# Gated delta rule: triangular blocks inverted by substitution on 16 rows instead of 32, without the trip through DRAM

## The chip, the cores and the metric

The kernel is one program on one core of one Trainium2 chip. It runs on TensorE (PE), VectorE (DVE), ScalarE (ACT), GpSimd (POOL) and SyncE (SP), which here only issues DMAs. The metric is the device time of one execution in microseconds, smaller is better; it is given as the median of several runs of the same kernel.

## The reference, cut to what matters

The reference is a chain of eight layers on an input of 1024 tokens by 256 features. The third, a gated delta rule with 6 heads (key width 32, value width 64), is the only one that the change touches. Per head it is

```
def _step(S, xs):
    qt, kt, vt, gt, bt = xs
    S = S * jnp.exp(gt)[..., None, None]
    pred = jnp.einsum('bhk,bhkv->bhv', kt, S)
    delta = (vt - pred) * bt[..., None]
    S = S + jnp.einsum('bhk,bhv->bhkv', kt, delta)
    return (S, jnp.einsum('bhk,bhkv->bhv', qt, S))
```

followed by a normalization, a gate and an output projection. The order is token by token. The kernel computes it in chunks of 128 tokens: 8 chunks a head, 48 in all. Within a chunk the tokens' corrections depend on each other through a strictly lower triangular 128x128 matrix A, and what is needed is the inverse T = (I - A)^-1 (A with its sign) of each of the 48. Then W = T times the scaled keys, and a scan over the 8 chunks carries the state.

## The kernel before, in words

`build` calls the layers one after the other, and each ends in a barrier of all engines. Inside a layer each `nc.Block` holds one instruction list per engine, and a block ends in a barrier too. Engines wait for each other by semaphores; all orders are written out by hand.

`gated_delta` has these blocks in order: projections and convolution (L1119); norms and decay factors (L1235); the block that makes A and the score matrices (L1347), where DVE subtracts and masks, ACT takes exponents and DVE multiplies with the products in PSUM (psum), two heads a step, while POOL scales keys, queries and values; the **inversion block** (L1461); the scan (L1597); the output norm (L1677); and `project_out`. EA holds the 48 matrices A, transposed, with keys on the partitions.

The inversion goes from small diagonal blocks to large ones.

*Substitution.* The 128 rows fall into four diagonal blocks of 32 (`group(q)`), so there are 192 blocks of 32x32. `load_a_blocks` (SP) writes the diagonal blocks to a DRAM scratch and reads them back so that each partition holds one whole block: 128 partitions for the first four heads (group 0), 64 for the last two (group 1). `substitute` then goes through the rows: step i multiplies column i of A with row i of T so far (an outer product, L1063) and adds it to the rows below (L1067), 31 steps of two instructions with waits between. DVE does group 0 while POOL does group 1. A copy transposes each block (L1070), and `store_t_blocks` and seven more DMAs take T and its transpose through DRAM to where TensorE wants them: TT (transposed inverse) and T64.

*Merges.* Two inverted neighbours T1, T2 with the block A21 between them give the lower left block T2 A21 T1. `x32` computes X = A21 T1 for the pairs of 32-row blocks, ACT copies X to SBUF, `y32` multiplies by T2, DVE copies into TT and T64; `x64` and `y64` do the same for the pair of 64-row blocks. All go in three batches b of 16 chunks, in the order x32(b), x64(b-1), y32(b), y64(b-1), W(b-2). A small matmul works on the tile of the 128x128 array that its operands' partitions name: rows by those of its inputs, columns by those of its output. float32 matmuls show as two records each in the trace.

*W.* `w_features(b)` (L1491) computes for each head and half four matmuls of 128 rows into 32 columns, so one column tile at a time; ACT copies the result with a minus sign (`keep_w`, nWT), and TensorE waits for every second copy.

The scan block (L1597) starts with SP loading `own_block`; DVE waits for it before its first copy of U (L1650).

## Time and profile before

| | |
|---|---|
| median of three runs | 1583.32 us (1582.37 to 1586.07) |
| the profiled execution | 1582.23 us |
| its span, first to last instruction | 1580.5 us |
| busy in the span: PE, DVE, ACT, POOL | 1351.1, 937.7, 670.4, 255.8 us |
| mean granted TensorE clock | 0.894 of full speed |
| the inversion block | 477.9 to 577.0 us of the span |

The profiled execution is 1.7 us longer than its span, and the median lies 1.1 us above the profiled execution. PE stands for matmuls and PEld for its weight loads. Busy shares are means over layers with different limits; what counts for one block is which engine or transfer ends last in it. A granted clock of 1.0 is 2.4 GHz, 0.5 is 1.2 GHz.

### The profile page before, as it was taken

To read this page: it belongs to the slowest core of one execution; us is meant where nothing else is said; L and a number is where in the kernel's file an instruction comes from. 1 tells how busy PE (TensorE), PEld (TensorE's weight loads), DVE (VectorE), ACT (ScalarE), POOL (GpSimd) and SP (SyncE) were. 2 spreads that over 40 slices of the span, in tenths; PEclk is the share of its full clock that TensorE was granted. 3 is DMA by queue.
4 is the path that set the end of the run, shared out by engine and by line. 5 is a ranking of instruction groups with operands and counts; after the bars stand their busy time and mean duration, and the time that the engine had idled before them with its cause. 6 is when DMAs were issued, how large, how long until landed. Compare 5 with 4: busy or idle time off the path is not lost. (4 is left out here: it accounts for less than half of the span.)

```text
span 1580.5 us, 31133 instructions
## 1 busy us (share of the span) xinstructions
PE 1351.1 (85%) x12875; PEld 756.3 (48%) x12883; DVE 937.7 (59%) x2142; ACT 670.4 (42%) x948; POOL 255.8 (16%) x340
## 2 busy tenths in 40 slices
PE   7999993987380696698999998999689999998999
PEld 3355542463250675456355545435335555555436
DVE  3899958644689125573899955442345555534331
ACT  4577773634331121463577773210334444442110
POOL 4300000000126202003300000120234343210110
PEclk9899996998555588799999998999869999998999
DMA  3122102000310400001222103000300000000000
GB/s 91 28 42 38 27 15 98 0 12 0 100 17 23 77 5 0 14 1 30 50 42 35 30 4 95 0 1 9 60 8 14 17 12 17 7 3 1 0 0 27
DMA packets 51807, 41.64 MB, mean 26 GB/s; under 512 B 26497, under 2 KB 41970, under 8 KB 51666
## 3 DMA queue, kind: packets, MB, share of 16 engines
q1 hardware_dynamic: 51666, 39.65, 11.6%
q8 instruction: 102, 1.67, 0.4%
q14 instruction: 39, 0.32, 0.1%
HBM read 20.33 MB, written 3.43 MB: 15 GB/s over the span
## 5 line engine op out<-in xcount | busy, mean ns | idle before, releaser
L560 DVE TENSOR_REDUCE row_max_pieces<-psum 128x1 f32<-128x512 f32 (+3 forms) x672 | 406.7, 647 | 121.2 <-PE psum L455 119.0
L657 ACT ACTIVATE probs<-psum 128x1024 f32<-128x1024 f32 (+7 forms) x384 | 343.5, 899 | 220.2 <-PE psum L455 220.1
L509 PE MATMUL psum<-probs,v_ones 128*32 128x256 f32 (+1 forms) x2688 | 238.7, 376 | 6.4 <-POOL probs L444 4.1
L455 PE MATMUL psum<-q_all,k_head 97*32 97x512 f32 (+3 forms) x1536 | 192.4, 492 | 3.5 <-issue 3.5
L455 PE MATMUL psum<-k_stack,q_stack 96*32 96x512 bf16 x2048 | 163.1, 388 | 4.7 <-DVE row_max_pieces L560 2.3
L455 PE MATMUL psum<-q_stack,k_stack 97*32 97x512 bf16 x2048 | 160.1, 384 | 0.0
L509 PEld LDWEIGHTS psum<-probs,v_ones 128*32 128x32 f32 x2688 | 88.2, 109 | 81.7 <-POOL probs L444 21.1
L455 PE MATMUL psum<-k_head_bf,q_all_bf 80*32 80x512 bf16 (+3 forms) x768 | 96.1, 346 | 4.8 <-POOL q_all_bf L2281 3.4
L455 PEld LDWEIGHTS psum<-q_all,k_head 97*32 97x32 f32 x1536 | 78.8, 110 | 34.4 <-issue 8.5
L455 PEld LDWEIGHTS psum<-k_stack,q_stack 96*32 96x32 bf16 x2048 | 57.4, 97 | 73.4 <-DVE row_max_pieces L560 20.5
L455 PEld LDWEIGHTS psum<-q_stack,k_stack 97*32 97x32 bf16 x2048 | 58.5, 97 | 51.4 <-ACT probs L657 3.7
L1873 PE MATMUL psum<-lora_in,arena 128*128 128x512 f32 (+1 forms) x192 | 80.0, 595 | 3.4 <-DVE lora_in L1951 3.4
L1963 DVE TENSOR_TENSOR gate_weighted<-psum,weight_rows 128x512 f32<-128x512 f32 (+1 forms) x48 | 33.2, 691 | 78.6 <-PE psum L1873 78.5
L1823 PE MATMUL psum<-xn_features,arena 128*128 128x512 f32 (+1 forms) x192 | 79.4, 594 | 0.0
L1905 ACT ACTIVATE silu<-psum 128x512 f32<-128x512 f32 x44 | 26.3, 597 | 118.6 <-PE psum L1873 118.6
L296 PE MATMUL psum<-xn_parts,w_up_signs 128*128 128x512 bf16 x186 | 48.2, 393 | 21.6 <-DVE xn_parts L345 21.4
L455 PEld LDWEIGHTS psum<-k_head_bf,q_all_bf 80*32 80x32 bf16 x768 | 37.2, 97 | 52.9 <-issue 26.5
L444 POOL TENSOR_SCALAR_AFFINE_SELECT probs<-probs 128x128 f32<-128x128 f32 x128 | 36.7, 290 | 112.8 <-ACT probs L657 112.8
L1873 PEld LDWEIGHTS psum<-lora_in,arena 128*128 128x128 f32 (+1 forms) x192 | 32.2, 181 | 46.8 <-issue 39.8
L1885 POOL TENSOR_TENSOR mixed_hidden<-slot_hidden 128x512 f32<-128x512 f32 x22 | 27.8, 1262 | 160.7 <-DVE slot_hidden L1968 160.7
L1823 PEld LDWEIGHTS psum<-xn_features,arena 128*128 128x128 f32 (+1 forms) x192 | 32.4, 181 | 42.3 <-issue 40.7
L2278 POOL TENSOR_TENSOR q_all<-by_cos_over_by_sin,by_sin_moved 64x512 f32<-64x512 f32 x32 | 40.6, 1269 | 69.1 <-DVE row_max_pieces L560 39.6
(321 smaller groups left out, 2068.9 us busy)
## 6 DMA issues: line engine op xcount, KB each, us to landing
q_stack<-arena SPq DMA_DIRECT2D x32, 96.0 KB, 2.7
k_stack<-arena SPq DMA_DIRECT2D x32, 96.0 KB, 2.7
arena<-gd_g_sums SPq DMA_DIRECT2D x6, 512.0 KB, 6.0
q_stack<-arena SPq DMA_DIRECT2D x32, 64.0 KB, 2.3
k_stack<-arena SPq DMA_DIRECT2D x32, 64.0 KB, 2.3
x_tokens<-in_x SPq DMA_DIRECT2D x4, 256.0 KB, 3.5
k_stack<-arena SPq DMA_DIRECT2D x32, 32.0 KB, 2.3
q_stack<-arena SPq DMA_DIRECT2D x32, 32.0 KB, 2.1
```

The source lines that it names most:

```text
L296: last = pe.matmul(psum[:, 2 * b + j, :], w[:, k, e * P:(e + 1) * P], XP[:, part, k, cols(half)], start=(part == 0 and k == 0), stop=(part ...
L444: pool.affine_select(out=own, in_=own, compare_op=ALU.is_ge, fill=0.0, base=0, pattern=[[1, P]], channel_multiplier=-1).then_inc(masked, 1)
L455: last = pe.matmul(o[j:j + 32], by[:, j:j + 32], rows, **flags)
L509: last = pe.matmul(psum[32 * g:32 * g + VW, PVB, a - g * D:D], V[:, c, h, :], pr[:, n % PB, a:(g + 1) * D], start=(c == 0), stop=(c == (2 ...
L560: last = dve.reduce_max(mx[:, h % 2, qt, i:i + 1], o[:, 0:plain], AX.X)
L657: act.activation(pr[:, n % PB, q_from(c):], psum[:, 2 * (n % 2):2 * (n % 2) + 2, :].rearrange("p a n -> p (a n)")[:, q_from(c):], ACT.Exp, ...
L1823: pe.matmul(psum[rows, 2 * (p % BUF) + j, :], w[wb][:, kk, features], XNT[:, kk, cols], start=(kk == 0), stop=False, skip_group_check=True)
L1873: last = pe.matmul(psum[rows, 2 * (p % BUF) + j, :], w[wl][:, features], Z[:, j, k, cols], start=False, stop=True, skip_group_check=True)
L1885: pool.tensor_tensor(MX[:, f, cols], H[:, 0, f, cols], H[:, 1, f, cols], ALU.add).then_inc(mixed, 1)
L1905: act.activation(sil[:, i % 2, :], psum[:, 2 * (p % BUF), :], ACT.Silu).then_inc(silu, 1)
L1963: last = dve.tensor_tensor(gc[rows, i % 2, :], psum[rows, 2 * (p % BUF) + 1, :], CB[rows, k, cols], ALU.mult)
L2278: pool.tensor_tensor(Q[0:RD, h % QSLOTS, cols(half)], t[0:RD, i % 3, :], moved[:, i % 3, :], ALU.add).then_inc(added, 1)
```

## The change

In words:

- *No DRAM.* `a_scratch`, `t_scratch`, `load_a_blocks` and `store_t_blocks` go. ACT packs the diagonal blocks of EA into AD (`compact_diagonals`, four ACTIVATEs of 32x512 per two heads: twice in the block that makes A, once in the inversion block). DVE transposes 32x32 blocks across partitions: `lay_a_blocks` before the substitution, `turn_t_blocks` (two) and `turn_rows` (one) behind it, for each of the two groups. AD is then T, and MA its transpose, with each block's own partitions, so the small matmuls read them there.
- *Substitution on 16 rows.* Each 32-row block is two diagonal blocks of 16, both in one instruction; 15 steps. DVE does both groups, on 128 partitions each (half of group 1 is zeros, which a POOL memset provides); POOL has nothing to do in this block.
- *One more level of merges.* `x16` and `y16` run over whole 32-row blocks with 16 columns, 64 matmuls each a batch on the four diagonal tiles of the array, `keep_x16` (ACT) copies X, and `add_y16` (DVE) adds Y to the rows from 16 up (`high_half` is one there, else zero).
- *A new order on TensorE*, with `x64(1, i)` and `y64(0, i)` alternating, and `keep_busy`: four 128x128x512 matmuls whose result is unused ahead of x16, two at the end.
- *W.* `w_features(f, half)` takes four heads (f = 0) or two (f = 1) in turn, each on its own column tile; ACT copies 128 or 64 rows at once.
- *Copies* into TT and T64 are now made by ACT (`place_rows`, `join_first`, `join`, one y64 copy) and DVE (`place_columns`, `join`, two y64 copies).
- *Moved.* The load of the output weights `wo` goes from the first block to the scan block, ahead of `own_block` on SP. `xn` of the output projection's norm lies in TT.

The diff, cut to its core:

```
+def compact_diagonals(act, pair):
+
+    n, s = slot_of(2 * NT * pair)
+    for q in range(4):
+        act.activation(AD[n][group(q), s:s + 2 * NT, :], EA[group(q), 2 * NT * pair:2 * NT * (pair + 1), group(q)],
+                       ACT.Copy).then_inc(compact[n], 1)
+
+def lay_a_blocks(dve, n):
+
+    dve.transpose(MA[n].rearrange("p j t -> p t j"), AD[n][:].rearrange("p c t -> p t c")).then_inc(laid[n], 1)
+
+def turn_t_blocks(dve, n):
+
+    dve.transpose(AD[n][:].rearrange("p c j -> p j c"), TB[n].rearrange("p t j -> p j t")
+                  ).then_inc(t_turned[n], 1)
+    dve.transpose(MA[n].rearrange("p c t -> p t c"), TB[n]).then_inc(t_turned[n], 1)
+
+def turn_rows(dve, n):
+
+    dve.transpose(MA[n].rearrange("p c t -> p (c t)"), AD[n][:].rearrange("p c j -> p (c j)")
+                  ).then_inc(t_turned[n], 1)
+
...
+def substitute(dve, n, steps):
+
+    step = swept[n]
+    a, t = diagonal(flat["minus_a_blocks"][n]), diagonal(flat["t_blocks"][n])
+    if 0 in steps:
+        dve.wait_ge(t_eye, 16 * NG)
+        dve.wait_ge(laid[n], 1)
+    for i in steps:
+        rows, cols = T16 - 1 - i, i + 1
+        prod = outer[:, 0:2 * rows * cols].rearrange("p (d t j) -> p d t j", d=2, j=cols)
         if i:
-            eng.wait_ge(step, 2 * i)
-        eng.tensor_tensor(prod, MA[n][:, i, i + 1:].unsqueeze(2).broadcast_to([blocks, rows, cols]),
-                          TB[n][:, i, 0:cols].unsqueeze(1).broadcast_to([blocks, rows, cols]),
+            dve.wait_ge(step, 2 * i)
+        dve.tensor_tensor(prod, a[:, :, i, i + 1:T16].unsqueeze(3).broadcast_to([P, 2, rows, cols]),
+                          t[:, :, i, 0:cols].unsqueeze(2).broadcast_to([P, 2, rows, cols]),
                           ALU.mult).then_inc(step, 1)
-        eng.wait_ge(step, 2 * i + 1)
-        eng.tensor_tensor(TB[n][:, i + 1:, 0:cols], TB[n][:, i + 1:, 0:cols], prod,
+        dve.wait_ge(step, 2 * i + 1)
+        dve.tensor_tensor(t[:, :, i + 1:, 0:cols], t[:, :, i + 1:, 0:cols], prod,
                           ALU.add).then_inc(step, 1)
-    eng.wait_ge(step, 2 * (T32 - 1))
-    eng.tensor_copy(MA[n][:], TB[n][:].rearrange("p t j -> p j t")).then_inc(step, 1)
-
-def load_a_blocks(sp, n):
-    for q in range(4):
-        sp.dma_start(a_scratch[n][q].rearrange("c j t -> j c t"), EA[group(q), chunks_of(n), group(q)]
-                     ).then_inc(a_written[n], 16)
-    sp.wait_ge(a_written[n], 64)
-    sp.dma_start(MA[n][:].rearrange("p j t -> p (j t)"), a_scratch[n].rearrange("q c j t -> (q c) (j t)")
-                 ).then_inc(a_loaded[n], 16)
-
-def store_t_blocks(sp, n):
-    sp.wait_ge(swept[n], 2 * T32 - 1)
-    for i, o in enumerate((MA, TB)):
-        sp.dma_start(t_scratch[n][i].rearrange("q c j t -> (q c) (j t)"),
-                     o[n][:].rearrange("p j t -> p (j t)")).then_inc(t_written[n], 16)
+    if T16 - 2 in steps:
+        dve.wait_ge(step, 2 * (T16 - 1))
...
-def load_a_blocks(sp, n):
-    for q in range(4):
-        sp.dma_start(a_scratch[n][q].rearrange("c j t -> j c t"), EA[group(q), chunks_of(n), group(q)]
-                     ).then_inc(a_written[n], 16)
-    sp.wait_ge(a_written[n], 64)
-    sp.dma_start(MA[n][:].rearrange("p j t -> p (j t)"), a_scratch[n].rearrange("q c j t -> (q c) (j t)")
-                 ).then_inc(a_loaded[n], 16)
-
-def store_t_blocks(sp, n):
-    sp.wait_ge(swept[n], 2 * T32 - 1)
-    for i, o in enumerate((MA, TB)):
-        sp.dma_start(t_scratch[n][i].rearrange("q c j t -> (q c) (j t)"),
-                     o[n][:].rearrange("p j t -> p (j t)")).then_inc(t_written[n], 16)
...
+                dve.tensor_reduce(high_half[:], ident[:].rearrange("p (q a) -> p q a", a=T32)[:, :, T16:],
+                                  AX.XY, ALU.add)
...
+            pool.memset(AD[1][:, GCH[1]:, :], 0.0)
...
+                if n in (5, 9):
+                    act.wait_ge(a_done, n - 1)
+                    compact_diagonals(act, n // 4 - 1)
...
+    def keep_busy(pe, bank_of, n):
+
+        for _ in range(n):
+            pe.matmul(psum[:, bank_of, :], ident[:], XNT[:, 0, 0:HALF], start=True, stop=True)
+
+    def keep_x16(act, b):
+        act.wait_ge(x16_in, b + 1)
+        act.activation(X16(b)[:, 0:CB * T16], psum[:, 2 * b, 0:CB * T16], ACT.Copy).then_inc(x16_kept, 1)
+
+    def add_y16(dve, b):
+
+        n, s = slot_of(b * CB)
+        dve.wait_ge(y16_in, b + 1)
+        o = AD[n][:, s:s + CB, 0:T16]
+        dve.scalar_tensor_tensor(o, sixteen(psum[:, 2 * b + 1, 0:CB * T16]), high_half[:, 0:1], o,
+                                 ALU.mult, ALU.add).then_inc(t32_done, 1)
+
+    def place_rows(copy, b, **kw):
+        n, s = slot_of(b * CB)
+        for q in (0, 1):
+            copy(T64[group(q), blk(b), group(q)], AD[n][group(q), s:s + CB, :], **kw).then_inc(rows_placed[b], 1)
+
+    def place_columns(copy, b, **kw):
+        n, s = slot_of(b * CB)
+        for q in range(4):
+            copy(TT[group(q), blk(b), group(q)], MA[n][group(q), s:s + CB, :], **kw).then_inc(columns_placed, 1)
+
+    def join_first(copy, b, **kw):
+        copy(T64[group(1), blk(b), group(0)], bank(b, 0)[group(1)], **kw).then_inc(joined_first, 1)
...
+            def w_features(f, half):
+
+                for b in (range(2), (2,))[f]:
+                    pe.wait_ge(y64_kept[b], 1)
+                    pe.wait_ge(joined[b], 2)
+                    pe.wait_ge(columns_placed, 4 * b + 4)
+                if f:
+                    pe.wait_ge(w_kept, half + 1)
+                for j in range(4):
+                    t = 4 * half + j
+                    for h in W_OF[f][0]:
+                        last = pe.matmul(psum[32 * (h % 4):32 * (h % 4) + 32, 6 + half, j * P:(j + 1) * P],
+                                         KBE[:, t, h, :], TT[:, h * NT + t, :], start=True, stop=True)
+                last.then_inc(w_in, 1)
+
+            def x16(b):
+                pe.wait_ge(t_turned[slot_of(b * CB)[0]], 1)
+                for i, c in enumerate(chunks(b)):
+                    for q in range(4):
+                        last = pe.matmul(psum[group(q), 2 * b, i * T16:(i + 1) * T16], EA[group(q), c, group(q)],
+                                         t_rows(q, c)[:, 0:T16], start=True, stop=True)
+                last.then_inc(x16_in, 1)
+
+            def y16(b):
+                pe.wait_ge(t_turned[slot_of(b * CB)[0]], 2)
+                pe.wait_ge(x16_kept, b + 1)
+                for i, c in enumerate(chunks(b)):
+                    for q in range(4):
+                        last = pe.matmul(psum[group(q), 2 * b + 1, i * T16:(i + 1) * T16], t_columns(q, c),
+                                         X16(b)[group(q), i * T16:(i + 1) * T16], start=True, stop=True)
+                last.then_inc(y16_in, 1)
...
+            pe.wait_ge(swept[0], T16)
+            keep_busy(pe, 6, kept_busy)
+            for stage in (x16, y16, x32, y32):
+                for b in range(2):
+                    stage(b)
+            x64_waits(0)
+            for i in range(CB):
+                x64(0, i)
+            x16(2)
+            x64_waits(1)
+            y64_waits(0)
+            for i in range(CB):
+                x64(1, i)
+                y64(0, i)
+            y16(2)
+            y64_waits(1)
+            for i in range(CB):
+                y64(1, i)
+            x32(2)
+            w_features(0, 0)
+            y32(2)
+            w_features(0, 1)
+            x64_waits(2)
+            for i in range(CB):
+                x64(2, i)
+            y64_waits(2)
+            for i in range(CB):
+                y64(2, i)
+            for half in range(NH2):
+                w_features(1, half)
+            keep_busy(pe, 0, kept_busy // 2)
...
+            copy = dict(func=ACT.Copy)
+            compact_diagonals(act, 2)
+            for o in (T64[group(0), :, group(1)], TT[group(1), :, group(0)], TT[group(3), :, group(2)],
+                      TT[hi, :, lo]):
                 rows, _, n = o.shape
                 act.activation(o, core.ones_sq[P - rows:, 0:n].unsqueeze(1).broadcast_to([rows, GH * NT, n]),
                                ACT.Copy, scale=0.0).then_inc(zeroed, 1)
-            for b in range(NBT + 2):
-                if b < NBT:
-                    act.wait_ge(x_in, b + 1)
-                    for q in (1, 3):
-                        act.activation(X32[group(q), b], bank(b, 0)[group(q)], ACT.Copy).then_inc(x_kept, 1)
-                if 1 <= b <= NBT:
-                    act.wait_ge(x64_in, b)
-                    act.activation(T64[hi, blk(b - 1)], half_bank(b - 1)[hi], ACT.Copy).then_inc(x64_kept, 1)
-                if b >= 2:
-                    keep_w(b - 2)
+            for b in range(2):
+                keep_x16(act, b)
+            for b in range(2):
+                act.wait_ge(t32_done, b + 1)
+                place_rows(act.activation, b, **copy)
+                keep_x32(b)
+            for b in range(2):
+                act.wait_ge(y_in, b + 1)
+                join_first(act.activation, b, **copy)
+                join(act.activation, b, **copy)
+            keep_x64(0)
+            keep_x16(act, 2)
+            keep_x64(1)
+            act.wait_ge(y64_in, 1)
+            act.activation(TT[lo, blk(0), hi], half_bank(0)[lo], ACT.Copy).then_inc(y64_kept[0], 1)
+            act.wait_ge(t32_done, 3)
+            place_rows(act.activation, 2, **copy)
+            keep_x32(2)
+            keep_w(0, 0)
+            act.wait_ge(y_in, 3)
+            join_first(act.activation, 2, **copy)
+            keep_w(0, 1)
+            keep_x64(2)
+            for half in range(NH2):
+                keep_w(1, half)
...
+            lay_a_blocks(dve, 0)
+            substitute(dve, 0, range(T16 - 1))
+            turn_t_blocks(dve, 0)
+            dve.wait_ge(compact[1], 4)
+            lay_a_blocks(dve, 1)
+            substitute(dve, 1, range(0, 6))
+            add_y16(dve, 0)
+            substitute(dve, 1, range(6, 11))
+            add_y16(dve, 1)
+            dve.wait_ge(t32_done, 2)
+            turn_rows(dve, 0)
+            substitute(dve, 1, range(11, T16 - 1))
+            turn_t_blocks(dve, 1)
+            dve.wait_ge(t_turned[0], 3)
+            for b in range(2):
+                place_columns(dve.tensor_copy, b)
+            add_y16(dve, 2)
+            dve.wait_ge(t32_done, 3)
+            turn_rows(dve, 1)
+            dve.wait_ge(t_turned[1], 3)
+            place_columns(dve.tensor_copy, 2)
+            dve.wait_ge(y64_in, 2)
+            dve.tensor_copy(TT[lo, blk(1), hi], half_bank(1)[lo]).then_inc(y64_kept[1], 1)
+            dve.wait_ge(y_in, 3)
+            join(dve.tensor_copy, 2)
+            dve.wait_ge(y64_in, 3)
+            dve.tensor_copy(TT[lo, blk(2), hi], half_bank(2)[lo]).then_inc(y64_kept[2], 1)
...
+            sp.dma_start(wo[:], d["wo"].rearrange("(k p) n -> p k n", p=P)).then_inc(wload, 16)
             sp.dma_start(own[:].rearrange("p a n -> p (a n)"), d["own"]).then_inc(own_in, 16)
+            sp.wait_ge(wload, 32)
```

## Rows read from the trace of the kernel before

**Rows 1.** Windows of the block: busy us (count) of PE, PEld, DVE, ACT, POOL; clock; DMA.

```profile
478.00:514.00 36.00, 0.00 (x0) 0.00 (x0) 33.10 (x63) 7.03 (x4) 25.92 (x44) 0.50 0.07 15
535.00:562.00 27.00, 26.78 (x410) 25.36 (x408) 6.54 (x8) 4.97 (x7) 0.00 (x0) 0.53 0.02 4
```

**Rows 2.** Timeline, TensorE: merges, W and the scan's start; [idle before <-releaser].

```profile
525.07 1.92 PE L1503 MATMUL psum<-t_first_half,arena 32*32 32x32 f32 x64 [50.35 <-DMA t_first_half<-gd_t_blocks]
528.29 1.75 PE L1510 MATMUL psum<-a_times_t,t_inverse_transposed 32*32 32x32 f32 x29 [1.30 <-ACT a_times_t L1563]
546.42 3.67 PE L1522 MATMUL psum<-t_first_half,arena 64*64 64x64 f32 x32
556.99 3.99 PE L1491 MATMUL psum<-t_inverse_transposed,k_beta_eg 128*32 128x128 f32 x24
562.20 2.08 PE L1522 MATMUL psum<-t_first_half,arena 64*64 64x64 f32 x32
577.08 1.52 PE L1615 MATMUL psum<-conv_tokens,t_inverse_transposed 128*128 128x64 f32 x12 [0.93 <-PEq L1461]
580.95 0.26 PEld L1627 LDWEIGHTS psum<-u,conv_tokens 128*32 128x32 f32 x12
580.96 0.42 PE L1627 MATMUL psum<-u,conv_tokens 128*32 128x64 f32 x12
```

**Rows 3.** Timeline, DVE: the substitution of the first group.

```profile
477.92 0.19 DVE L1063 TENSOR_TENSOR outer_products<-minus_a_blocks,t_blocks 128x31 f32<-128x31 f32 x1 [0.39 <-PEq L1347]
478.39 0.22 DVE L1063 TENSOR_TENSOR outer_products<-minus_a_blocks,t_blocks 128x60 f32<-128x60 f32 x1
480.76 0.32 DVE L1063 TENSOR_TENSOR outer_products<-minus_a_blocks,t_blocks 128x156 f32<-128x156 f32 x1
481.47 0.34 DVE L1063 TENSOR_TENSOR outer_products<-minus_a_blocks,t_blocks 128x175 f32<-128x175 f32 x1
510.34 0.69 DVE L1063 TENSOR_TENSOR outer_products<-minus_a_blocks,t_blocks 128x31 f32<-128x31 f32 x1
511.72 1.50 DVE L1070 COPY minus_a_blocks<-t_blocks 128x1024 f32<-128x1024 f32 x1
```

**Rows 4.** Groups by form, 477 to 578 us: xcount | busy us, mean ns of one.

```profile
L1563 ACT ACTIVATE a_times_t<-psum 32x512 f32<-32x512 f32 x6 | 3.5, 588 | 54.9 <-PE psum L1503 54.8
L1566 ACT ACTIVATE t_first_half<-psum 64x1024 f32<-64x1024 f32 x3 | 3.1, 1018 | 7.0 <-PE psum L1522 7.0
L1582 DVE COPY t_inverse_transposed<-psum 64x1024 f32<-64x1024 f32 x3 | 3.7, 1217 | 12.3 <-PE psum L1528 12.3
```

**Rows 5.** Timeline, weight loads of 512-column matmuls after an idle stretch.

```profile
346.11 0.34 PEld L1140 LDWEIGHTS psum<-xn_features,arena 128*128 128x128 f32 x1 [0.52 <-issue]
346.96 0.34 PEld L1140 LDWEIGHTS psum<-xn_features,arena 128*128 128x128 f32 x1 [0.52 <-issue]
```

**Rows 6.** Windows of 1 us: where the clock rises and falls (columns as above).

```profile
560.00:561.00 1.00, 0.98 (x11) 0.68 (x6) 0.00 (x0) 0.43 (x1) 0.00 (x0) 0.84 0.00 0
567.00:568.00 1.00, 1.00 (x11) 0.81 (x10) 0.35 (x1) 0.00 (x0) 0.00 (x0) 0.57 0.00 0
```

**Rows 7.** Groups by form, POOL: a memset.

```profile
L853 POOL MEMSET v_ones<- 128x1920 f32 x2 | 3.4, 1698 | 111.0 <-POOLq L70 98.4 <-POOLq L158 12.6
```

**Rows 8.** Timeline, the block before: DVE beside POOL, ACT's exponents.

```profile
429.25 14.89 DVE L1425 SCALAR_TENSOR_TENSOR arena<-arena,g_sums,zero_or_masked 128x128 f32<-128x128 f32 x8 [1.97 <-POOL zero_or_masked L1355]
459.59 1.14 ACT L1411 ACTIVATE arena<-arena 128x512 f32<-128x512 f32 x2
462.87 0.69 DVE L1433 TENSOR_TENSOR p_by_key<-psum,arena 128x512 f32<-128x512 f32 x1 [0.17 <-PE psum L1386]
```

**Rows 9.** Timeline, DVE: the first copy of U in the scan.

```profile
579.68 0.56 DVE L1650 COPY u<-psum 128x384 f32<-128x384 f32 x1 [1.30 <-PE psum L1606]
```

**Rows 10.** DMA issues: KB each, median us to landing.

```profile
own_block<-in_g_own SPq DMA_DIRECT2D x1, 128.0 KB, 2.0
delta_wo<-in_g_wo SPq DMA_DIRECT2D x1, 384.0 KB, 3.2
```

188 lines of the change are left out of this document (76 added, 112 removed).

## The prediction

> **What bounds the kernel now.** I read the windows first, to see which stretch the change touches and which engine works in it. The kernel is one chain of layers, and the gated delta's inversion block runs from 477.9 to 577.0 us: 99.2 us from its first DVE instruction to the first matmul of the scan behind it, at 577.08 [rows 1 to 3]. TensorE does nothing in the first 36 us of it, and from 535 to 562 it is full (26.8 of 27.0 us), at a granted clock of 0.53. The reader is to see three different limits in a row: DVE, DMA, TensorE.
>
> Next the timeline of TensorE, for what it was idle for: the mark behind its first matmul says 50.35 us until the transfer that brings the blocks back from DRAM [rows 2]. Behind that transfer stands the substitution, 31 steps of a multiply and an add. DVE's timeline prices them [rows 3]: DVE starts a step of 31 elements 0.47 us before the next one; one of 156 elements takes 0.71 us (480.76 to 481.47). From then on POOL works as well, and DVE's last multiply, again only 31 elements, lasts 0.69 us where the first took 0.19. The DVE ends at 513.2 after its 1.50 us copy, and another 11.8 us go by with two trips through DRAM before the first 32-row merge at 525.07. Nothing else of the kernel overlaps this block, since every layer waits for the last one; what is saved in it is saved at the end.
>
> **What the change does to this block.** I count from the block's start.
>
> *Substitution.* Two diagonal blocks of 16 rows go in one instruction, in 15 steps instead of 31; step i has 2(15-i)(i+1) elements, 1360 in all. From the two rows the step costs 0.41 us + 1.92 ns per element, so 15 x 0.41 + 1360 x 0.00192 = 8.8 us. This takes DVE's pace before POOL joined; POOL has no work in the new block. The Trainium skill (SBUF — State Buffer, Who interferes with whom) says a Vector instruction with two SBUF inputs blocks against a GpSimd one that reads SBUF; by it the late pace is POOL's doing and the 8.8 us stand. Were the late pace DVE's own (two of 0.69 us, 1.4 us a step), the first group would take 21 us, 12 more; the same 31 elements at 0.19 and 0.69 us speak against it, but other things differ between these rows, so it stays in the range.
>
> *Transposes.* lay_a_blocks and turn_t_blocks are DVE transposes of 128x1024; the trace has none. The nearest rows are a straight copy of 1024 columns at 1.22 us [rows 4], below, and the rearranging copy of the same shape at 1.50 us [rows 3], with POOL beside it, above; since no row shows a transpose I keep 4 us, some three copies, as the far bound. I take 1.3 us, near the copies. One lies before the substitution and one behind it ahead of the first matmul: first data at 1.3 + 8.8 + 1.3 = 11.4 us. At 4 us each, this start and the later turns add about 8 us.
>
> *keep_busy.* Four 512-column matmuls are released after 8 steps: 1.3 + 4.7 = 6.0 us (744 elements). A matmul is two records, and the weight loads show 0.85 us per 512-column record at half clock [rows 5], so 6.8 us if the clock stays. It rose at 560.3, 3.3 us after the 128-row matmuls began at 556.99 [rows 2, 6]; the same here would give 5.1 us. I take 5.8: TensorE is free at 11.8. This costs 0.4 us and runs mostly in TensorE's idle time.
>
> *X and Y of 16 rows.* New work: for each third, 64 small matmuls twice, 128 records a stage. The 32-row X stages give a record on two alternating tiles every 30 ns at half clock (64 in 1.92 us) while one tile alone takes 60 ns (29 in 1.75 us) [rows 2]. At full clock twelve records on four column tiles load in 0.26 us, 22 ns each. The new ones are half as wide and go over four tiles, so arithmetic doesn't bind, the issue does: 3.6 us a stage at 28 ns, 2.9 at 22. Two of the six right behind keep_busy at 2.9, four at 3.6: 20.2 us. All six at 22 ns would give 2.8 us back.
>
> *32-row stages.* The matmuls stay, 3 x 1.9 + 3 x 3.2 = 15.3 us, fed straight from the transposed tiles.
>
> *64-row stages.* Sixteen matmuls take 3.67 us at half clock, 2.08 at full [rows 2]. Before there were six in a row. Now X of the second third alternates with Y of the first on different rows and columns, which should overlap as the two 32-row tiles do: 4 x 3.65 + 3.7 = 18.3 us. No overlap: 3.6 more.
>
> *W.* Four heads on four column tiles: 16 matmuls a call, four after another in each tile, 4 x 2 x 0.213 = 1.75 us at half clock; six heads' small matmuls in 0.42 us (twelve records) [rows 2] show the column tiles overlap. The last two calls have two tiles and as many steps: 4 x 1.75 = 7.0 us.
>
> *Waits left on TensorE's path.* Most copies hide behind other thirds. At the end, where one third is left, keep_x64 (1.02 us) and the last Y copy (1.22) lie open [rows 4]: with hand-over 2.4 us. I followed ACT too: its 2.4 us of compaction and the zero fill that it had before end ahead of the first X, and each X or Y copy of 32 rows is two or three of 0.59 us behind another stage. The last keep_busy, two matmuls, ends in rising clock: 2.6 us, only 0.6 of it under keep_w. Barrier 0.3.
>
> Sum: 11.8 + 20.2 + 15.3 + 18.3 + 7.0 + 2.4 + 2.6 + 0.3 = 77.9 us, against 99.2: 21.3 saved. Of it the DRAM trips are the largest part, the shorter steps the next, and about 20 us of new small matmuls eat much of both.
>
> **The clock** decides how much more. It stayed at 0.50 all through the 32- and 64-row stages until 560, rose in W, and fell at 567.1 after 5 us of 64-row work [rows 1, 6]. The new block is nearly all such narrow work, so I price it at half.
>
> **What it adds outside.** POOL's memset of 512 columns goes ahead of the mask for which DVE waits already (1.97 us), and DVE's next eight instructions, between POOL's, last until 444.1, so what POOL is late they are late: from a memset of 1920 columns in 1.70 us, 0.45 us, say 0.5 [rows 7, 8]. ACT's compaction (4 x 0.6 us) behind the sixth exponent pushes the seventh, which ends at 460.73 before, to 463.1, where DVE wants it at 462.87: 0.2 us [rows 8]. The second compaction ends before it is missed. The third is in the new block, counted. The output weights' load moves to the scan and goes ahead of own_block in SP's queue: alone own_block lands 2.0 us after issue and the weights 3.2 [rows 10], so behind them it lands near 580.7 on the old axis instead of 579.0, and DVE, which waits for it ahead of its copy of U at 579.68 [rows 9], is 1.0 us late; between nothing and 1.7. Behind that wait are all of DVE's scan steps, once. The weights themselves are wanted 65 us later. Identity rows and the sum of ident are hidden under loads and the projection. The shared xn changes no instruction. Together +1.7 us.
>
> So 21.3 - 1.7 = 19.6 us saved: span 1580.5 to 1560.9; the profiled run was 1.7 us above its span and the median of three 1.1 above that: 1563.7, I say 1563.5.
>
> **Rivals.**
> A, *the clock stays up*. If keep_busy and the alternating stages hold it, 64-row stages take 2.1, W 0.9, small stages 2.9, 32-row ones 1.5 and 2.3: the same walk ends at 62 us, or 1548. For it: the clock did hold for 5 us over 64-row work. Against: it then fell, and it never rose in 32 us of it. Chance 0.12, in between cases included.
> B, *dearer DVE work*: transposes at 4 us (+8), or steps at POOL-time pace (+12), the merges unchanged: 1571 to 1577. Chance 0.14.
> C, *slower than before*: the 16-row records, 768 in all, do not overlap and cost the 60 ns of a single tile. Six stages then take 46 us instead of 20.2, the block 103.8, the kernel 1589. It decides from 52 ns a record on. Against it the 30 ns on two tiles. Chance 0.07. The Trainium skill (TensorEngine Tiling, Instruction Overhead) speaks for it: about 60 cycles a matmul, a free size of 1 no quicker than 60. That would be 50 ns at 1.2 GHz, 6.4 us a stage and an estimate of 1582, no change; the 30 ns records of 32 columns at that clock disagree.
> D, *nothing gained*: C in part (about 50 ns), or B and no overlap at once; within 0.2% (3 us, about what a measurement of this kernel can tell from no change). Chance 0.03.
> The likeliest case has 0.64 and its own range, 1557 to 1570: small stages at 22 or 30 ns, overlap of the 64s or none, own_block 0 to 1.7.
> The full range, 1550 to 1577, takes in most of A and B. Faster 0.64 + 0.12 + 0.14 = 0.90, same 0.03, slower 0.07.
>
> **What the profile after would show.** The block's start to the scan's first matmul in 78 us; fifteen steps of 0.47 to 0.66 us; transposes of 1.3 us; 64 small matmuls in 3 to 3.6 us; the granted clock at 1.0 around 10 to 15 us into the block, 0.5 through most of the merges, 1.0 again by the scan; x64 and y64 rows alternating within 3.7 us together; DVE waiting for own_block's load ahead of the first copy of U. Wrong would be: the clock at 1.0 through the merges (lower), transposes of many microseconds or records 50 ns apart (higher), or TensorE waiting on DVE between the stages, which I found nowhere but at 0 to 11 and near the end.

## The result, and the profile after

The changed kernel takes 1591.9 us, median of five runs (1589.5 to 1597.6), against 1583.3 for the kernel before in the same rounds: ratio 1.0052, with a 95% interval from 1.0033 to 1.007. It is slower by 8.6 us, where 1563.5 was forecast, within 1550 to 1577. The profiled run of it was the slowest of the five: 1597.6 us, span 1595.8.

The first thing to look at is the block that was changed. These are rows of TensorE's timeline in the changed kernel, from the filler of `keep_busy` to the scan (start, duration, what, count, and in brackets the idle time before it and what ended it); they answer to [rows 2].

```profile
483.31 5.60 PE L1492 MATMUL psum<-xn_features,identity 128*128 128x512 f32 x8 [9.85 <-DVE t_blocks L1094]
489.32 1.41 PE L1545 MATMUL psum<-diagonal_blocks,arena 32*32 32x16 f32 x146 [0.40 <-DVE diagonal_blocks L1065]
492.70 1.10 PE L1545 MATMUL psum<-diagonal_blocks,arena 32*32 32x16 f32 x110 [1.97 <-issue]
...
496.55 1.89 PE L1554 MATMUL psum<-a_times_t,minus_a_blocks 32*32 32x16 f32 x127 [2.55 <-issue]
...
513.10 3.67 PE L1586 MATMUL psum<-t_first_half,arena 64*64 64x64 f32 x32
...
518.53 0.36 PE L1586 MATMUL psum<-t_first_half,arena 64*64 64x64 f32 x1
518.54 0.36 PE L1596 MATMUL psum<-t_inverse_transposed,t_first_half 64*64 64x64 f32 x1
...
521.79 1.09 PE L1554 MATMUL psum<-a_times_t,minus_a_blocks 32*32 32x16 f32 x109
...
547.44 3.63 PE L1537 MATMUL psum<-t_inverse_transposed,k_beta_eg 128*32 128x128 f32 x32 [1.31 <-DVE t_inverse_transposed L1710]
551.00 2.48 PE L1492 MATMUL psum<-xn_features,identity 128*128 128x512 f32 x4
553.78 1.52 PE L1746 MATMUL psum<-conv_tokens,t_inverse_transposed 128*128 128x64 f32 x12 [0.30 <-PEq L1523]
...
559.82 0.64 PE L1758 MATMUL psum<-u,conv_tokens 128*32 128x64 f32 x12 [2.10 <-DVE u L1781]
```

And DVE's timeline, the block's start and the copies of U in the scan [rows 3, 9].

```profile
476.59 1.93 DVE L1061 STREAM_TRANSPOSE minus_a_blocks<-diagonal_blocks 128x1024 f32<-128x1024 f32 x1 [0.32 <-PEq L1361]
478.62 0.19 DVE L1090 TENSOR_TENSOR outer_products<-minus_a_blocks,t_blocks 128x30 f32<-128x30 f32 x1
...
487.29 1.97 DVE L1065 STREAM_TRANSPOSE diagonal_blocks<-t_blocks 128x1024 f32<-128x1024 f32 x1
...
559.21 0.56 DVE L1781 COPY u<-psum 128x384 f32<-128x384 f32 x1 [4.13 <-DMA own_block<-in_g_own]
566.81 0.56 DVE L1781 COPY u<-psum 128x384 f32<-128x384 f32 x1 [5.18 <-PE psum L1737]
576.44 0.56 DVE L1781 COPY u<-psum 128x384 f32<-128x384 f32 x1 [5.12 <-PE psum L1737]
```

From DVE's first instruction at 476.59 to the scan's first matmul at 553.78 the block takes 77.2 us. It took 99.2, and 77.9 was forecast. So 22 us were saved in the block, and more was lost behind it: from the scan's first matmul to its end it takes 77.3 us, where it took 43.5. The rest of the kernel behind the scan took 964.7 us in this profiled run and 959.9 in the one before; runs of one kernel scatter by as much, and I read nothing from it. The DVE copies say where: the scan's steps are 9.63 us apart (566.81 to 576.44), to the end of the scan, where those of before were 5.26 apart. Three windows of 1 us at the scan's start, and one over most of it, say why (busy us and count of PE, PEld, DVE, ACT, POOL, then the granted clock):

```profile
557.00:558.00 1.00, 0.72 (x7) 0.58 (x6) 0.00 (x0) 0.00 (x0) 0.00 (x0) 1.00 0.06 8
558.00:559.00 1.00, 0.00 (x0) 0.00 (x0) 0.00 (x0) 0.00 (x0) 0.00 (x0) 0.93 0.04 14
559.00:560.00 1.00, 0.18 (x8) 0.18 (x10) 0.56 (x1) 0.00 (x0) 0.00 (x0) 0.50 0.00 0
560.00:630.00 70.00, 69.35 (x324) 54.31 (x319) 12.55 (x39) 3.44 (x7) 0.00 (x0) 0.50 0.00 0
```

TensorE runs out of work at 557.7, because the kernel lets DVE copy the first U only behind its wait for own_block. In its 2.1 us of idle the granted clock goes from 1.0 to 0.5. Then TensorE is 99% busy for 70 us and the clock stays at 0.50. The two loads at the scan's start, to be read beside [rows 10] (KB each, us from issue to landing):

```profile
delta_wo<-in_g_wo SPq DMA_DIRECT2D x1, 384.0 KB, 5.1
own_block<-in_g_own SPq DMA_DIRECT2D x1, 128.0 KB, 5.0
```

own_block took 2.0 us before. So the reading is: the load that moved ahead of own_block makes DVE wait, the wait makes TensorE idle, the idle costs the clock, and the scan doesn't get it back. The experiments test each link of this, and then the parts of the block.

### The profile page after: what moved, and what is told of

Read it like the earlier page. It is cut to its first block and busy times, and to the rows that moved or that the text cites. A ratio compares the mean times of both kernels' runs of the same rounds, so it can differ in the third digit from the quotient of the medians.

```text
span 1595.8 us, 32658 instructions
## 1 busy us (share of the span) xinstructions
PE 1394.2 (87%) x13655; PEld 789.2 (49%) x13663; DVE 933.8 (59%) x2155; ACT 683.9 (43%) x969; POOL 220.7 (14%) x278
## 3 DMA queue, kind: packets, MB, share of 16 engines
HBM read 18.43 MB, written 1.07 MB: 12 GB/s over the span
## 5 line engine op out<-in xcount | busy, mean ns | idle before, releaser
L444 POOL TENSOR_SCALAR_AFFINE_SELECT probs<-probs 128x128 f32<-128x128 f32 x128 | 36.7, 290 | 116.6 <-ACT probs L657 116.6
```

The lines of the kernel that those rows point to most:

```text
L444: pool.affine_select(out=own, in_=own, compare_op=ALU.is_ge, fill=0.0, base=0, pattern=[[1, P]], channel_multiplier=-1).then_inc(masked, 1)
```

## The experiments

Each group of four ran on one chip beside the kernel before. Runs of one kernel scatter by some 4 us to either side there, and by up to 9, so terms of 1 us are read from traces and not from medians. In the profiled runs of the changed kernel and its variants the inversion block begins at different times (its filler starts anywhere from 477.7 to 487.2), though most of the edits come behind that place; I compare lengths counted inside the block.

### Own_block first

Theory: the order of two loads makes the whole difference between forecast and result.

```
 def _(sp):
+    sp.dma_start(own[:]..., d["own"]).then_inc(own_in, 16)
     sp.dma_start(wo[:], ...).then_inc(wload, 16)
-    sp.dma_start(own[:]..., d["own"]).then_inc(own_in, 16)
     sp.wait_ge(wload, 32)
```

> The changed kernel with one line moved: the load of own_block is issued ahead of the load of the output weights. Theory A (the wait for own_block idles TensorE at the scan's start, the clock falls and the scan stays at the low level): DVE's first copy of U no longer waits for the load, the granted clock is 1.0 through the scan, the scan takes about 44 us instead of 77, and the kernel ends 31 to 36 us earlier than the changed one, about 1560 us (the block's 77 us kept). Rival B (the clock is too fresh after the narrow merges and falls in the scan whatever the load does): the wait of 4 us goes, the clock still falls to 0.5, the time drops by 2 to 5 us, to about 1588.

Measured: 1560.9 us (1554.0 to 1566.3), before 1581.6; ratio 0.9856, interval 0.9829 to 0.9884. own_block lands in 2.1 us. The DVE rows of this version, and a window over its scan:

```profile
555.77 0.56 DVE L1781 COPY u<-psum 128x384 f32<-128x384 f32 x1 [1.30 <-PE psum L1737]
560.93 0.56 DVE L1781 COPY u<-psum 128x384 f32<-128x384 f32 x1 [2.30 <-PE psum L1737]
```

```profile
557.00:596.00 39.00, 38.24 (x326) 30.14 (x324) 12.57 (x39) 3.51 (x8) 0.00 (x0) 1.00 0.00 1
```

The first copy waits for TensorE again (1.30 us, as in [rows 9]), and the clock is 1.00 for 39 us. Swapping two lines is worth some 30 us against the changed kernel (the ratios to the kernel before are 1.0052 and 0.9856). The traces account for it: the eight copies of U span 36.7 us here (555.77 to 592.48) and 65.4 in the changed kernel (559.21 to 624.61), 28.7 more, and the first is 2.8 us later after the scan's first matmul.

### The wait where it is needed

The changed kernel with its loads in its own order, and DVE's wait for own_block moved from the scan's start to its first read of it, ahead of the products into SD.

```
 dve.wait_ge(s0, 1)
-dve.wait_ge(own_in, 16)
 dve.wait_ge(blocked, 2)
 ...
+    if t == 0:
+        dve.wait_ge(own_in, 16)
     for f, (w, nh) in enumerate(WID):
         dve.tensor_tensor(SD[...], St[...]..., own[0:w, 0:nh, :], ALU.mult)...
```

> The changed kernel with the loads in its own order, but DVE waits for own_block only where it first reads it, after the first two state updates. The load lands at the same time, so DVE's wait there is about 1 us instead of 4 us, and TensorE's idle time is short. Theory A: the clock holds, the scan takes 45 us, the kernel about 1561 us. Rival B: the clock falls all the same, about 1588 us.

Measured: 1560.7 us (1555.5 to 1563.4), ratio 0.9865, interval 0.9835 to 0.9896. The one row of DVE's timeline that waits for the load:

```profile
558.66 0.62 DVE L1794 TENSOR_TENSOR arena<-state,own_block 128x256 f32<-128x256 f32 x2 [0.56 <-DMA own_block<-in_g_own]
```

own_block still lands 4.9 us after its issue, and the wait for it is down to 0.56 us. TensorE has no idle at its first read of U, and the granted clock is 1.00 from 552 to 562 with no filler in the scan. The late transfer alone costs nothing; the wait placed ahead of work that didn't need it did.

### The same wait, with TensorE kept at work

Is it the wait or TensorE's idle in it? Here the wait stays, and three matmuls on a free PSUM bank stand where TensorE would be idle.

```
     u_from_v(t + 1)
+if t == 0:
+    for _ in range(3):
+        pe.matmul(psum[:, 6, :], ident[:], TT[:, 0:4, :], start=True, stop=True)
 pe.wait_ge(u_kept, t + 1)
```

> The changed kernel with its loads in its own order (wo ahead of own_block), and three matmuls of the identity by 512 columns put on TensorE in the scan's first step, just where it idles for the copy of U that own_block's load delays. Theory A (it is TensorE's idle in that wait that brings the clock to 0.5, and the wait itself is cheap): the wait for own_block stays, DVE still copies the first U some 4 us late, the clock stays at 1.0, scan steps are 5.26 us apart, and the time is that of the version with own_block loaded first, 1560.9, plus about 3 us of wait: 1564, between 1561 and 1567. Rival B (the collision of the two loads, or the late start of the scan, does it in another way, with the idle only a companion): the clock falls all the same, steps of 9.6 us, 1592 to 1594.

Measured: 1560.7 us (1558.3 to 1564.2), before 1581.4; ratio 0.9874, interval 0.9843 to 0.9906. First DVE, then TensorE:

```profile
556.41 0.56 DVE L1784 COPY u<-psum 128x384 f32<-128x384 f32 x1 [3.94 <-DMA own_block<-in_g_own]
561.57 0.56 DVE L1784 COPY u<-psum 128x384 f32<-128x384 f32 x1 [2.30 <-PE psum L1737]
```

```profile
554.96 2.79 PE L1757 MATMUL psum<-t_inverse_transposed,identity 128*128 128x512 f32 x6
557.68 0.42 PE L1761 MATMUL psum<-u,conv_tokens 128*32 128x64 f32 x12
```

DVE waits as long as in the changed kernel (3.94 against 4.13 us), and the next step follows after 5.16 us. Only TensorE's idle was taken away, with 2.8 us of filler (three matmuls, six records), and some 30 us came back. The granted clock never leaves 1.00 from 550 to 562. This is the run that separates wait and idle. By itself it leaves open whether the filler holds the clock by ending the idle or by being full-size work; the version above, without idle and without filler, says that the absence of the idle is enough. The 3 us that were expected for the wait don't show in the median; in the trace the stretch from the scan's first matmul to its last copy of U is 2.6 us longer than with own_block first (41.9 against 39.3).

### The load alone, in the kernel before

```
-sp.dma_start(wo[:], ...).then_inc(wload, 16)        # in loads(sp)
 ...
+sp.dma_start(wo[:], ...).then_inc(wload, 16)        # in the scan, ahead of own
 sp.dma_start(own[:]..., d["own"]).then_inc(own_in, 16)
```

> The kernel before with only the load of the output weights moved to the scan, ahead of own_block. Theory A: own_block lands some 5 us after its issue, DVE waits for it some 2.5 us past the time that it copies U now, TensorE is idle meanwhile and the clock falls; the scan takes about 77 us instead of 44 and the kernel about 1615 us. Rival B (the fall needs the new merges ahead): the clock was already at 1.0 for 6 us at the scan's start and stays; only the wait itself is added, 1585 to 1587 us.

Measured: 1581.5 us; nine of ten runs within 1575.7 to 1584.5, one at 1609.8. Ratio 0.999, interval 0.9972 to 1.0008. DVE and TensorE at the scan's start:

```profile
583.12 0.56 DVE L1651 COPY u<-psum 128x384 f32<-128x384 f32 x1 [2.37 <-DMA own_block<-in_g_own]
```

```profile
583.73 0.42 PE L1628 MATMUL psum<-u,conv_tokens 128*32 128x64 f32 x12 [0.33 <-DVE u L1651]
```

Here own_block landed in 3.2 us, DVE waited 1.07 us longer than in [rows 9], TensorE was idle for 0.33 us, and the clock stayed at 1.0. That is the forecast's price of the moved load, 1.0 us, and nothing else. Both theories had counted on a load of some 5 us, so neither was tested by this run. The same edit has two prices, then, by whether TensorE's own work lasts until the load is there. The single run at 1609.8 (mean granted clock 0.878, where the others have 0.894 or more) has the size of a scan at half clock; there is no trace of it.

### A longer wait in the kernel before

If the idle is the cause, the kernel before must fall too when its wait is made longer. The load of wo comes twice, the second time to a spare tile.

```
 sp.dma_start(wo[:], ...).then_inc(wload, 16)
+sp.dma_start(spare[:], ...).then_inc(wload, 16)
 sp.dma_start(own[:]..., d["own"]).then_inc(own_in, 16)
```

> The kernel before with wo's load moved to the scan and loaded twice (the second time to a spare tile) ahead of own_block: all work of the inversion as before, with a longer wait for own_block at the scan's start. With one such load own_block landed 3.2 us after its issue and the clock stayed up in most runs. Theory A (a long enough idle of TensorE there brings the clock down, in any kernel, and the scan then stays down): own_block lands 5 to 6 us after its issue, TensorE is idle for 2 us or more, the scan's steps are 9.6 us apart, and the time is about 1581.5 + 2 + 28, some 1611. Rival B (only a clock that has just risen, as in the changed kernel, can be lost so; here it has been up for long): steps of 5.26 us, 1581.5 + 2, about 1584.

Measured: 1613.3 us (1607.8 to 1614.6), ratio 1.0192, interval 1.0155 to 1.0229. DVE, and TensorE's first matmul that reads U:

```profile
579.34 0.56 DVE L1653 COPY u<-psum 128x384 f32<-128x384 f32 x1 [4.80 <-DMA own_block<-in_g_own]
586.72 0.56 DVE L1653 COPY u<-psum 128x384 f32<-128x384 f32 x1 [5.18 <-PE psum L1609]
596.35 0.56 DVE L1653 COPY u<-psum 128x384 f32<-128x384 f32 x1 [5.11 <-PE psum L1609]
```

```profile
579.96 0.42 PE L1630 MATMUL psum<-u,conv_tokens 128*32 128x64 f32 x12 [2.77 <-DVE u L1653]
```

```profile
580.00:581.00 1.00, 1.00 (x16) 0.91 (x16) 0.55 (x3) 0.00 (x0) 0.00 (x0) 0.65 0.02 8
```

With none of the change's arithmetic in it, the kernel before loses 32 us: 2.77 us of idle, then steps 9.63 us apart (586.72 to 596.35), and the granted clock is 0.50 from 581 to 645. It had been at 1.0 for 11 us when the idle began, against 6 us in the changed kernel. So neither the new block nor so short a time at 1.0 is needed. The window shows one thing more: the clock is still 1.00 through the whole idle (577.2 to 579.96) and falls at 580.3, when TensorE is at work again.

### Entering the scan at the low clock

The version with own_block first, without the two matmuls of `keep_busy` at the block's end.

```
 for half in range(NH2):
     w_features(1, half)
-keep_busy(pe, 0, kept_busy // 2)
```

> As the first run, and without the two keep_busy matmuls at the end of the inversion block. If a scan keeps the level that it starts with (theory A in its strong form), TensorE enters it at 0.5 and stays there: about 1590 us. If 128-row matmuls without a gap are enough to raise the clock, as in W before, it rises in the first microseconds of the scan and the time is about 1559 to 1561 us, 1 us below the first run or the same.

Measured: median 1590.2 us; nine of ten runs lie within 1584.8 to 1596.7, and one is at 1556.2. Its DVE rows:

```profile
565.31 0.56 DVE L1780 COPY u<-psum 128x384 f32<-128x384 f32 x1 [5.18 <-PE psum L1736]
574.94 0.56 DVE L1780 COPY u<-psum 128x384 f32<-128x384 f32 x1 [5.11 <-PE psum L1736]
```

own_block is there before DVE asks for it, yet the steps are 9.63 us apart, and the granted clock is 0.50 from the scan's first matmul on. The scan can be entered at either level and mostly keeps it: the time is around 1590 or 1556, and nothing lies between. The run at 1556.2 has a mean granted clock of 0.903, the others 0.877 to 0.885; why it alone rose isn't known, as there is no trace of it. In the other versions the 2.5 us of filler at the block's end bring the clock up ahead of the scan.

### Raising the clock in the middle of the scan

The changed kernel, untouched until t = 3; there six filler matmuls stand in the place that three had above.

> The changed kernel with six matmuls of the identity by 512 columns put on TensorE in the scan's fourth step (t = 3), while the scan runs at a granted clock of 0.5. Theory A (the scan keeps the level at which it runs, low or high, and full matmuls without a gap raise it): the clock goes to 1.0 in the filler or just behind it, the steps behind are 5.26 us apart and not 9.63, four to four and a half steps save 17.5 to 19.7 us, the filler costs 6 to 8 us, and the time is 1591.9 less 10 to 14, about 1580. Rival B (the scan's own instructions hold the clock low once it is low, whatever stands between): steps of 9.6 us to the end, the filler adds 8 us, 1600. Rival C (it rises and falls again in a step or two): between, about 1592 to 1595.

Measured: 1579.4 us (1574.6 to 1586.5), before 1581.4; ratio 0.9993, interval 0.997 to 1.0015. A window in the filler, then DVE's copies around it:

```profile
583.00:584.00 1.00, 1.00 (x3) 0.44 (x2) 0.00 (x0) 0.00 (x0) 0.00 (x0) 0.83 0.00 0
```

```profile
578.05 0.56 DVE L1784 COPY u<-psum 128x384 f32<-128x384 f32 x1 [5.11 <-PE psum L1737]
591.12 0.56 DVE L1784 COPY u<-psum 128x384 f32<-128x384 f32 x1 [2.23 <-PE psum L1737]
596.38 0.56 DVE L1784 COPY u<-psum 128x384 f32<-128x384 f32 x1 [2.23 <-PE psum L1737]
```

The clock rises inside the filler, and the last steps are 5.26 us apart with it. The scan's own 99% busy had not raised it in the 25 us before, nor in the 70 us of the changed kernel. The filler costs 3.4 us in its own step (13.07 against 9.63) and saves about 4.4 in each later one.

The scan's start in this version is that of the changed kernel, so it is a second sample of how the clock is lost. TensorE's row, and two windows:

```profile
553.76 0.42 PE L1761 MATMUL psum<-u,conv_tokens 128*32 128x64 f32 x12 [1.78 <-DVE u L1784]
```

```profile
555.00:556.00 1.00, 1.00 (x8) 0.75 (x7) 0.35 (x2) 0.00 (x0) 0.00 (x0) 1.00 0.00 0
556.00:557.00 1.00, 1.00 (x4) 0.70 (x4) 0.00 (x0) 0.09 (x1) 0.00 (x0) 0.51 0.00 0
```

Here the idle is 1.78 us and the clock holds through it and for 2.2 us of work behind it, before it falls. Whoever looks only at the window of the idle misses the fall.

### Twice as many small matmuls

Why do the stages on 16 rows take what they take? Their bursts are short, and between them TensorE is idle for about 2 us with the mark `issue`, which means that the profile shows nothing waited for. The base is the version with own_block first.

```
 def x16(b):
     pe.wait_ge(t_turned[slot_of(b * CB)[0]], 1)
-    for i, c in enumerate(chunks(b)):
+    for i, c in [(i, c) for _ in range(1 + (b < 2)) for i, c in enumerate(chunks(b))]:
```

> The version with own_block loaded first (1560.9 us) with the matmuls of x16(0) and x16(1) each issued twice, 128 more of 32 rows by 16 columns in each. Theory A (in these stages TensorE waits for its instructions: the gaps of 1.5 to 2.5 us after every 256 or so instructions are their supply): each further 128 matmuls cost a burst and a gap, about 3.15 us, so the time rises by about 6.3 us, to 1567. Rival B (the gaps belong to the changes of stage and the copies between them, not to the number of instructions): only the bursts are paid, 1.4 us each, 2.8 us in all, 1563.7. Rival C (the stages wait for something else that the doubled matmuls run beside): nothing, 1561.

Measured: 1566.4 us (1564.6 to 1569.4), ratio 0.9899, interval 0.9868 to 0.993. TensorE's timeline:

```profile
487.54 1.41 PE L1545 MATMUL psum<-diagonal_blocks,arena 32*32 32x16 f32 x146 [0.48 <-DVE diagonal_blocks L1065]
491.19 1.40 PE L1545 MATMUL psum<-diagonal_blocks,arena 32*32 32x16 f32 x128 [2.24 <-issue]
494.92 1.90 PE L1545 MATMUL psum<-diagonal_blocks,arena 32*32 32x16 f32 x128 [2.33 <-issue]
498.37 1.63 PE L1545 MATMUL psum<-diagonal_blocks,arena 32*32 32x16 f32 x108 [1.55 <-issue]
```

Now all four bursts belong to one loop with no copy or change of stage between them, and the gaps are there as before. From the first of these matmuls to the scan's first it takes 71.5 us (487.54 to 559.06), against 64.2 and 64.9 in the two profiled runs of the base: 6.6 to 7.3 more, near the 6.3 expected from supply, far from the 2.8 of the bursts. The changed kernel's DMA view has a row for the loading of instructions (484 to 510 us; packets, MB, share of 16 engines):

```profile
q8 instruction: 6, 0.10, 1.7%
```

Six packets with 0.10 MB are some 16 KB each, and the bursts there begin every 3.4 to 3.9 us, 128 matmul records and as many weight loads apart: one packet a burst. The packets don't move in the gaps: in windows of 0.25 us each falls late in a burst (490.25, 493.5, 497.5, 501.5), and the next burst begins 2.1 to 3.1 us behind it. So TensorE executes a burst faster than its next instructions come; that it is this packet for which a burst waits is read from the counts and the doubled loop, and no row names it. The Trainium skill (Advanced Engine Details and Errata, ISA Cache) gives 16 KB as a line of 256 instructions, and this agrees with both counts. It also says (Runtime: NRT & Kernel Launch, Instruction fetch mechanics) that crossing such a boundary is mostly hidden; with matmuls of 16 columns on four tiles the traces here disagree: where such bursts follow each other, 1.4 to 2.6 us lie open between them.

### Without the filler at the start

```
 pe.wait_ge(swept[0], T16)
-keep_busy(pe, 6, kept_busy)
```

> The version with own_block loaded first, without the four matmuls of identity by 512 columns that the changed kernel issues during the substitution. Theory A (the stages on 16 rows wait for their instructions, so the level of the clock there is worth nothing): the clock stays at 0.5 through them, each burst takes 1.9 instead of 1.4 us and each gap that much less, and the time is that of the base within 1 us: 1560 to 1562. Rival B (the filler works as the forecast priced it, 2.9 against 3.6 us a stage in the two or three stages at full clock): 1.4 to 2.1 us slower, 1562.5. Rival C (without it the clock is also lost at a later place, such as the scan): 1590.

Measured: 1561.2 us (1559.3 to 1566.1), ratio 0.9888, interval 0.986 to 0.9916; the base in the same group took 1564.8 (below). TensorE:

```profile
486.91 2.28 PE L1545 MATMUL psum<-diagonal_blocks,arena 32*32 32x16 f32 x154 [15.88 <-DVE diagonal_blocks L1065]
490.66 1.53 PE L1545 MATMUL psum<-diagonal_blocks,arena 32*32 32x16 f32 x99 [1.47 <-issue]
```

The bursts are longer and the gaps shorter, and the second burst comes 3.75 us after the first, as with the filler (3.65). From the first small matmul to the scan it takes 63.2 us, and the whole block 75.9, against 77.0 and 77.6 in the two profiled runs of the base: no longer than with it. The median can't part this from rival B (1562.5); these lengths do. The filler at the start buys nothing, because instructions and not the clock set the pace there.

### X and Y of 64 rows one after the other

```
 for i in range(CB):
     x64(1, i)
-    y64(0, i)
+for i in range(CB):
+    y64(0, i)
```

> The version with own_block loaded first, with x64(1) issued whole and y64(0) whole behind it instead of alternating. Theory A (as forecast, the two of a pair run beside each other, and the order is worth one stage at half clock): 3.7 us slower, 1564.6. Rival B (the pair already ran half overlapped or the stage is bounded by the instructions' supply): under 1.5 us.

Measured: 1566.6 us (1558.8 to 1568.1 in three runs, one at 1601.4), ratio 0.9882, interval 0.9847 to 0.9917. The median can't tell this from the base. The run at 1601.4 has a mean granted clock of 0.876, like a scan at half clock, and no trace; so a version with own_block first isn't proof against it. For the rest the timeline can tell:

```profile
520.04 3.35 PE L1586 MATMUL psum<-t_first_half,arena 64*64 64x64 f32 x29
...
526.68 1.90 PE L1554 MATMUL psum<-a_times_t,minus_a_blocks 32*32 32x16 f32 x128
```

The two stages take 6.6 us (520.04 to 526.68) where the alternating pair takes 3.3 (518.53 to 521.79 in the changed kernel, where the clock rises at its end) or 3.6 (in the second run of the base, at half clock throughout): the overlap is real. But y16(2) behind it then runs without a gap, in 1.8 us and not 3.0 to 3.3, so over a third is given back, and from the first small matmul to the scan the version takes 65.9 us against 64.2 and 64.9. The order is worth 1.0 to 1.6 us of the 3.7 forecast: rival B's size, by the supply of instructions and not by a half overlap.

### Both remedies, and the base again

Both edits of the first two experiments in one kernel, and a second run of the first.

> Both remedies at once: own_block loaded ahead of wo, and DVE waits for it only at its first read of it. Theory A (each alone leaves nothing of the wait on TensorE's path): same as either alone, 1560 to 1561, with DVE's first copy of U ended by TensorE alone. Rival B (some of the wait for own_block still counted in the version with only the order changed): 0.5 to 1 us less than that, 1560.

Measured: 1561.9 us (1557.4 to 1564.1), ratio 0.9875, interval 0.9852 to 0.9897.

> The version with own_block loaded first once more, as the base of this group of runs: 1560.9 us as in the first group, within 1.5 us, with the clock at 1.0 through the scan. A share of runs near 1590 would say that this version too can lose the clock.

Measured: 1564.8 us (1560.4 to 1566.9), ratio 0.9893, interval 0.9865 to 0.9921. The second run of the base lies 3.9 us above the first, outside the 1.5 us expected, though its four mean granted clocks (0.898 to 0.904) say that none of its runs lost the clock. Medians of this kernel scatter by that much. The intervals of all the versions that keep the clock overlap, so the remedies can't be told apart. Their ratios lie 1.1 to 1.4% below the kernel before, and 1.6 to 2.0 points below the change as given.

## Why the prediction was wrong

**The step that failed** is the price of the moved load: "DVE, which waits for it ahead of its copy of U at 579.68, is 1.0 us late; between nothing and 1.7." I carried that lateness to DVE's steps and not to TensorE, so the sum had +1.0 us where the runs showed some 30. It was mis-sized too: own_block landed in 5.0 us, not some 3.7, and the first U was 2.8 us late. With a linear price that would have been an error of 1.8 us. But the wait left TensorE idle for 2.1 us, the granted clock fell, and the scan, 43.5 us long before, took 77. "1.0 again by the scan" was true at 553 and false at 560. Nothing in the sum or the rivals had a path from a wait to the clock of the stage behind it. Both errors were needed. Had own_block landed in the 3.7 us of the forecast, U would have been ready 0.3 us after TensorE needed it, by the forecast's own rows; that is the case of the kernel before with the load moved (idle 0.33 us), which kept its clock. With own_block first the kernel takes 1560.9, which is the forecast of 1563.5 within the scatter, 20.7 us below the kernel before beside it, where the forecast's block saved 21.3 less 0.7 for the other terms.

**The rows that could have said so** were there. TensorE has 3.9 us of work at the scan's start before it needs the first U (577.08 to 580.96 [rows 2]), and the clock was lost once in that trace already. I laid its fall at 567.1 [rows 6] to 5 us of 64-row work, and passed over what stands in the middle of that work:

```profile
565.38 2.23 PE L1528 MATMUL psum<-t_inverse_transposed,t_first_half 64*64 64x64 f32 x32 [1.11 <-ACT t_first_half L1566]
```

The fall came 1.7 us behind the end of an idle of 1.11 us. Whether the idle or the narrow work brought it there, no run separates. I asked when DVE would be late, and not what TensorE would have left to do by then.

**Rival C gave nearly the time**, 1589, by luck: its mechanism was wrong. Records of 16 columns didn't cost TensorE 60 ns each: 128 of them took 1.90 us at half clock, 15 ns each. They go to the four tiles in turn, so on one tile one starts every 60 ns, as those of 32 columns did; what the rival had wrong is that they don't overlap. The rule of about 60 cycles a matmul (the Trainium skill, TensorEngine Tiling, Instruction Overhead), which stood beside that rival, is not what the trace shows if it is read as a cost to the whole engine; as a cost to each tile these rows don't contradict it.

**The sum, term by term** (forecast, then changed kernel):
- first small matmul 11.8, measured 12.7. The substitution took 8.7 as worked out; multiplies of 30 elements took 0.19 us first (478.62) and last (486.84), so POOL-time pace (rival B) didn't come. The rearranging transposes took 1.93 and 1.97, not 1.3.
- six stages on 16 rows 20.2, measured 17.6; bounded by the supply of instructions and not, as argued, by a cost of each record.
- 32-row stages 15.3, measured 16.6, with one of the supply gaps in them.
- 64-row stages 18.3, measured 17.8; W 7.0, measured 7.3; open copies 2.4 and 2.4; tail 2.6 and 2.5; barrier 0.3 and 0.3.

The measured ones come to 77.2. Two errors of more than 1 us had opposite signs; the sum is closer than its parts. The clock in the block ran as said: up from the filler until 494, then 0.5 but for 521 to 525 until the tail, so rival A fell. The small terms ahead of the block (POOL's memset took 0.52 us, as said) drown in the 9.5 us by which its start varies between profiled runs (470.9 to 480.5).

## What to carry to other kernels

A wait is priced by the idle that it leaves on TensorE, and an idle is priced by the stage behind it: ask at which clock that stage will run, and for how long nothing will raise it. Look for the fall in the microseconds behind the idle too, not only in it. A load moved to a block's start belongs behind those for which that block waits first, and a wait belongs at the first read. Where a long stage of small matmuls is entered, a few microseconds of full-size filler ahead of it, or in its first gap, are cheap against half speed all through: 2.5 and 2.8 us here against some 30. And matmuls too small for the supply of their own instructions are priced by their number, not by clock or columns.

## What the runs showed of the hardware that was not expected

- TensorE's granted clock doesn't follow the busy share of the profile. The same scan ran 99% busy for 70 us at 0.50, and 98% busy for 39 us at 1.00; six matmuls of 512 columns moved it from one to the other. In the profiled runs an idle of 1.78, of 2.10 and of 2.77 us at the scan's start was followed by the low level, one of 0.33 us was not. No bound between these was measured.
- The fall comes at no fixed point of the idle: it came 1.1 us into it in the changed kernel, 0.3 us behind its end in the kernel before with the longer wait, and 2.2 us behind its end in the version with filler in the middle.
- Where the small matmuls follow each other, TensorE runs blocks of about 256 instructions (128 matmul records and their weight loads) that begin 3.0 to 4.0 us apart, at either level of the clock.
- A transpose of 128x1024 on DVE takes 1.25 us with contiguous input and output (L1071) and 1.85 to 1.97 us with input or output rearranged (L1061 to L1067). The changed kernel's groups by form (busy, mean ns of one, idle before):

```profile
L1061 DVE STREAM_TRANSPOSE minus_a_blocks<-arena 128x1024 f32<-128x1024 f32 x1 | 1.8, 1849 | 0.0
L1071 DVE STREAM_TRANSPOSE minus_a_blocks<-diagonal_blocks 128x1024 f32<-128x1024 f32 x1 | 1.2, 1245 | 0.0
```

- Behind the 384 KB load the 128 KB load landed after 4.7 to 5.0 us in the changed kernel and its variants and after 3.2 in the kernel before, and the 384 KB load itself after 4.8 to 5.1 and 3.3. Why the same two transfers take longer there wasn't settled.
